# Self attention of a decoder layer: queries and keys projected in tiles of 128 tokens that run over batch borders

## What is computed

```python
# x: 8 batches x 224 tokens x 512; 16 heads of 64
x = rmsnorm(tokens) * norm_w
q, k, v = x @ Wq, x @ Wk, x @ Wv                 # heads split
q = q / max(norm(q), 1e-12) * (q_gamma + 1) * 8  # per token and head
k = k / max(norm(k), 1e-12) * (k_gamma + 1) * 8
sim = tanh(q @ k.T / 50) * 50 / 8
out = softmax(sim) @ v @ Wo                      # within a batch
x1 = layernorm(tokens + out)
```

## Time and profile before

| what | us |
|---|---|
| three executions | 1809.39, 1807.59, 1807.08 |
| their median | 1807.59 |
| the profiled execution | 1808.88 |
| its span, first to last instruction | 1806.4 |
| PE busy in the span | 1752.7 (97%) |
| DVE, ACT, POOL busy | 1412.5, 1172.5, 1113.4 |

### The profile page before, as it was taken

How to read it: one execution, slowest core, us unless ns; L and a number is a source line. 1 busy time by engine, 2 the same in 40 slices (tenths; PEclk the granted TensorE clock), 3 DMA queues, 4 the chain that set the end, 5 groups by cost and what they waited for, 6 DMA issues and landing times.

```text
span 1806.4 us, 37455 instructions
## 1 busy us (share of the span) xinstructions
PE 1752.7 (97%) x13942; PEld 1475.7 (82%) x13957; DVE 1412.5 (78%) x3240; ACT 1172.5 (65%) x2680; POOL 1113.4 (62%) x1250
## 2 busy tenths in 40 slices
PE   8999999999998899999999999999999999988997
PEld 7777777778877899999999999899899999974443
DVE  6777778787887677777777788777776777787888
ACT  6878887756755566666666667666666656654664
POOL 3434445664566586786686655677777788551554
PEclk9999999999998999999999999999999999999999
DMA  5223323111105423432432523314313341543553
GB/s 206 76 67 94 103 75 111 46 32 46 48 22 173 137 90 98 152 100 77 153 103 74 167 97 86 112 49 125 96 61 101 96 114 52 125 106 92 129 129 97
DMA packets 141106, 176.80 MB, mean 98 GB/s; under 512 B 63884, under 2 KB 99088, under 8 KB 140928
## 3 DMA queue, kind: packets, MB, share of 16 engines
q1 hardware_dynamic: 122392, 138.15, 25.3%
q0 software_dynamic: 14656, 28.92, 5.9%
q10 hardware_dynamic: 3880, 7.35, 1.3%
HBM read 109.25 MB, written 50.46 MB: 88 GB/s over the span
## 4 chain that ended last, share of the span: by engine, by line
PE 74%; DVE 10%; ACT 5%; POOL 5%; DMA 3%; issue 3%; ACTq 0%; POOLq 0%; DVEq 0%
PE att_ps_T L552 7%; PE att_ps_SA L1755 5%; PE att_ps_P L1731 5%; PE att_ps_SB L612 4%; PE att_ps_P L1719 4%; PE att_ps_P L552 4%; PE att_ps_P L1783 4%; PE att_ps_SB L600 3%; PE att_ps_O L1719 3%; PE att_ps_T L1719 3%; PE att_ps_P L1769 3%; PE att_ps_T L1731 3%; PE att_ps_O L1731 2%; PE att_ps_P L1794 2%; POOL sa_p_lo L423 2%
## 5 line engine op out<-in xcount | busy, mean ns | idle before, releaser
L1537 POOL TENSOR_TENSOR ca_pr<-ca_pr,ca_rec 112x750 f32<-112x750 f32 x256 | 366.6, 1453 | 187.2 <-DVE ca_rec L2017 184.3
L423 POOL TENSOR_TENSOR sa_p_lo<-sa_pr,sa_p_hi 112x448 fp32r<-112x448 f32 x128 | 146.8, 1162 | 210.5 <-ACT sa_p_hi L718 209.7
L1902 ACT ACTIVATE ca_big<-att_ps_P 126x384 fp32r<-126x384 f32 (+1 forms) x254 | 105.3, 449 | 66.1 <-PE att_ps_P L1769 64.9
L1896 ACT ACTIVATE ca_pr<-att_ps_SA,ca_nmax 112x750 f32<-112x750 f32 x128 | 113.7, 888 | 22.0 <-DVE ca_nmax L2013 11.2
L887 DVE RECIPROCAL sa_sums<-sa_sums 128x224 f32<-128x224 f32 x64 | 99.1, 1548 | 33.8 <-ACT sa_sums L727 33.6
L2022 DVE TENSOR_TENSOR ca_big<-att_ps_P,ca_big 126x384 fp32r<-126x384 f32 (+1 forms) x254 | 119.8, 498 | 6.2 <-ACT ca_big L1902 5.9
L2013 DVE TENSOR_REDUCE ca_nmax<-att_ps_SA 112x1 f32<-112x752 f32 x128 | 119.1, 931 | 1.3 <-PE att_ps_SA L1755 1.2
L2013 DVE TENSOR_REDUCE ca_nmax<-att_ps_SB 112x1 f32<-112x752 f32 x128 | 119.1, 930 | 0.0
L1731 PE MATMUL att_ps_P<-ca_w_hi,ca_ct 128*126 128x256 f32 x558 | 114.2, 284 | 1.4 <-DVE ca_q_lo L1996 1.4
L1896 ACT ACTIVATE ca_pr<-att_ps_SB,ca_nmax 112x750 f32<-112x750 f32 x128 | 113.3, 885 | 0.1
L1769 PEld LDWEIGHTS att_ps_P<-att_ident,ca_pr 64*126 64x126 f32 (+1 forms) x1524 | 85.5, 138 | 15.2 <-issue 10.8
(11 more groups left out here) (354 smaller groups left out, 6618.9 us busy)
## 6 DMA issues: line engine op xcount, KB each, us to landing
ct_kept<-ca_ct SPq DMA_DIRECT2D x8, 1134.0 KB, 9.3
ca_ct<-ct_kept POOLq DMA_DIRECT2D x8, 1134.0 KB, 7.7
ct_kept<-ca_ct SPq DMA_DIRECT2D x8, 1116.0 KB, 12.3
ca_ct<-ct_kept POOLq DMA_DIRECT2D x8, 1116.0 KB, 10.0
sa_xin<-in_x_dram SPq DMA_DIRECT2D x16, 448.0 KB, 3.7
xt_kept<-ca_xt SPq DMA_DIRECT2D x8, 896.0 KB, 5.2
ca_xt<-xt_kept POOLq DMA_DIRECT2D x8, 896.0 KB, 5.3
ternary<-ca_stage SPq DMA_DIRECT2D x36, 172.0 KB, 1.9
```

The costliest lines, as they stand in the source:

```text
L423: pool.tensor_tensor(p_lo[:, h % NB, :], pr[:, h % NB, :], f32(p_hi[:, h % NB, :]), ALU.subtract).then_inc(p_split, 1)
L1537: pool.tensor_tensor(w, w, rec[:, h % PB, c:c + 1].to_broadcast([R, S]), ALU.mult).then_inc(norm_done, 1)
L1896: act.activation(pr[:, h % PB, c, :].rearrange("r (a s) -> r a s", a=2), two_halves(psum[slot]), ACT.Exp, bias=nmax[:, h % PB, c:c + 1], a ...
```

## The change

Queries and keys are projected in tiles of P = 128 tokens counted over all 8 batches of a group, so four batches (896 tokens) are 7 tiles instead of 8. Within each four, the batches take up tiles [0, 1], [2, 3], [4, 5] and [6] (`TILES_OF`); for the fourth (batches 3, 7, 11, 15) the units Q1 and K1, their squares, sums, links of the norm and scalings are left out, and the engine only advances the semaphore. Values stay in tiles of 112 tokens of one batch.

- A tile can reach into the next batch. So x is transposed one batch earlier: AHEAD is 3, X and its splits are +++, and Q1 also waits for the next batch's XT0 and XT1. xt_hi and xt_lo become rings of two batches (448 columns and 64 more; the 64 are a second copy of the start of batches 2, 6, 10, 14, `wraps`).
- q_hi, q_lo, k_hi, k_lo become rings of two batches. T writes 128 columns per tile. For batches 1, 5, 9, 13 the two tiles run over the ring's end, and each copy is two pieces (`RING_PIECES`).
- guard is per tile, so the squares ss of the rows must come into the tiles' partitions: SP moves them with 3 or 4 small DMAs per batch in group 0 (`spread_squares`) ahead of the load of the next x, and DVE makes the guards from them in a new item U++ of its table (`guards`). guard is kept for group 1.
- sq has 2 places for 4, th 2 for 4, p_lo is written in the place of pr.
- The first two weight blocks' w_lo and gammas move on DVE from ahead of HQ0 of batch 0 to ahead of XT0 of batch 1; loads of group 1's first two weight blocks move on SP from behind x[1] to behind x[2].

```diff
-    AHEAD = 2
+    AHEAD = 3
+    PERIOD = 4
+    XW = 2 * N + HALF
+    TILES_IN = PERIOD * N // P
+    TILE_COLUMNS = [[0, P], [2 * P, 3 * P], [HALF, HALF + P], [2 * P + HALF]]
+    TILES_OF = [[0, 1], [2, 3], [4, 5], [6]]
+    TILES_READY = [[0], [1, 2], [3, 4], [5, 6]]
+    RING_PIECES = [[(0, 0, 2 * P)], [(0, 2 * P, P + HALF), (P + HALF, 0, HALF)], [(0, HALF, 2 * P)], [(0, 2 * P + HALF, P)]]
...
+        def spread_squares(m):
+            for c, r, n, t, row in pieces_of(m):
+                sp.dma_start(tile_ss[row:row + n, t:t + 1], ss[r:r + n, m % 2, c:c + 1]).then_inc(ss_spread, 16)
...
         def load_rows(src, before):
             if before:
+                sp.wait_ge(ss_done, before(2, 2))
+                if number(before) < B:
+                    spread_squares(number(before))
                 sp.wait_ge(filled[slot["XT1"]], filled_count("XT1", before))
-                sp.wait_ge(ss_done, before(2, 2))
...
             if b == 1:
                 load_weights(0, range(2, 4))
+            elif b == 2:
                 load_weights(1, range(2))
...
+            if u[0] != "V" and c >= len(tiles(at)):
+                pe.sem_inc(filled[slot[u]], 1)
+                return
...
+            if u == "Q1":
+                for t in range(2):
+                    pe.wait_ge(drained[slot[f"XT{t}"]], drained_count(f"XT{t}", lambda per, k: at(per, k) + per))
...
-                mm = pe.matmul(ps(u)[0:R, :], xs[:, k, c * R:c * R + R], ws[i][:, k, :],
+                mm = pe.matmul(ps(u)[0:rows, :], xs[:, k, col:col + rows], ws[i][:, k, :],
...
-                for c in range(2):
-                    mm = pe.transpose(ps(u)[:, i * N + c * R:i * N + c * R + R], t[:, c, p * P:p * P + P], ident[0:R, 0:R])
+                for c in range(len(tiles(at))):
+                    col = (2 * i + c) * P
+                    mm = pe.transpose(ps(u)[:, col:col + P], t[:, c, p * P:p * P + P], ident[:, :])
...
-            act.activation(q_hi[:, p, :], ps(u)[:, 0:N], ACT.Copy).then_inc(t_hi_done, 1)
+            for start, to, width in RING_PIECES[number(at) % PERIOD]:
+                q = act.activation(q_hi[:, p, to:to + width], ps(u)[:, start:start + width], ACT.Copy)
+            q.then_inc(t_hi_done, 1)
...
+            if wraps(u, at):
+                act.activation(xt_hi[:, :, 2 * N:XW], x_blocks(u)[:, :, 0, :], ACT.Copy)
...
+            dve.wait_ge(ss_spread, spread_count(m))
+            dve.tensor_scalar(guard[:, of], tile_ss[:, of], 1e-24 / DM, 1e-24 * RMS_EPS, ALU.mult, ALU.add).then_inc(guard_done, 1)
...
-                        if name == "HQ0":
-                            weights_lo(0)
-                            weights_lo(1)
-                            gammas()
-                        elif name == "G":
+                        if name == "G":
                             small_weights()
+                    if isinstance(b, int) and g * B + b + n == 1 and name == "XT0":
+                        weights_lo(0)
+                        weights_lo(1)
+                        gammas()
```

211 lines of the change are left out of this document (143 added, 68 removed).

## The result

The changed kernel takes 1830.11 us (median of four executions, 1824.19 to 1835.74), the kernel before beside it 1808.49. The ratio is 1.0115, 95% interval 1.0096 to 1.0135. The direction was forecast; 1816.5 was not the size, and the range ended at 1826. The profiled execution took 1830.53 us with a span of 1828.7, 22.3 more than before.

A forecast was written before the change was run, and what follows sets the result against it. In self attention the chain S3, ACT, POOL, O7 was taken to be as long as PE's stretch and to set it. Terms -9.9 + 3.1 + 8.8 + 2 + 5 = +9.0 us, forecast 1816.5 beside 1807.59, range 1803 to 1826.

The forecast's parts named there:

- The tiles, -9.9: Self attention's four steps without Q1 and K1: only K1's absence pays, 2.7 us each in group 0, 2.25 in group 1.
- V0 starts at 123.89 where K1 starts now: Step 2 of group 0: without K1, V0 takes its start time and Y0 has no stall, gain 2.7 us.
- The clock, +5: Four new PE gaps of some 2.2 to 2.7 us likely bring half clock: 5 us lost (0 to 12).
- Pieces and copies, +3.1: Copies of q and k split at the ring's end, 2.1 us, and extra x copies, 0.25 each: 3.1 lost (0 to 6).
- The start, +8.8 and +2: Kernel's start: waits on small DMAs, weights and x[2] delay K0's square, 8.8 us; K1 at half clock adds 2.
- (d): Start: ACT does x[2]'s squares ahead of Q0's and K0's, so K0's square ends at 26.5, not 17.74: 8.8 us.
- Term (a): Start: DVE waits for three small DMAs ahead of copying wnorm (at 10.7), holding ACT's first weight split, now at 7.22.
- term (e): Start: PE idles from about 22 to K1 at 30.8, so K1 runs at half clock: 2 us lost (0 to 2.8).
- The first: Rival: the clock holds in the short steps' gaps, +4.0 us, 1811.6; chance 0.15.
- The second: Rival: cheap start, small DMAs pass the weights, K1 stays fast, 6.5 us for 10.8, 1812.3; chance 0.12.
- The third: Rival: ACT or POOL serve heads 6 and 7 sooner, PE gains all 22.2 us, 1799.3; chance 0.08.
- The fourth: Rival: long clock falls behind the gaps, +12 us for +5, 1823.6; chance 0.10.

The follow-up runs named there:

- b4: Kernel before, Q1 and K1 of batches 3, 7, 11, 15 left out, ones in Q1's place, K0 scaled ahead of the third pair in group 1's short steps; 1809.32 us.
- b5: Same as b4, but the tiles left out are those of batches 2, 6, 10 and 14; 1802.11 us.
- e7: Changed kernel with ones in Q1's place and, in group 1's short steps, DVE scaling K0 right behind Q0; 1826.43 us.
- e1: Changed kernel plus ten matmuls of ones on PE wherever Q1 does not exist; 1829.39 us.
- b2: Kernel before, Q1 and K1 of batches 3, 7, 11, 15 left out, ten matmuls of ones in each missing Q1's place; 1809.99 us.
- b3: Kernel before, with ACT's and DVE's copies of q and k of batches 1, 5, 9, 13 each done in two pieces; 1810.97 us.
- e3: Changed kernel, with ACT taking the squares of x[2] behind batch 0's first V copy, not ahead of Q0's and K0's first squares; 1823.15 us.
- e5: e4 plus DVE scaling K0 right behind Q0 in group 1's short steps, and 20 more records of ones ahead of the first transposes of q; 1815.79 us.
- e6: e5 with POOL making the first two w_hi pieces for group 1's V weights behind the first head's p_lo in step 6; 1819.31 us.
- e4: Changed kernel with the edits of e1, e2 and e3 together, and the ones ahead of Q0 moved ahead of x[1]'s transposes; 1819.34 us.
- e2: Changed kernel, with DVE copying wnorm ahead of the guard of batch 0 instead of behind it; 1826.86 us.
- b1: Kernel before, Q1 and K1 of batches 3, 7, 11, 15 left out and nothing else; 1811.29 us.

## Why the prediction was right in direction and wrong in size

- *The tiles, -9.9.* Right in its mechanism for group 0, and Q1 is worth nothing: with the gap filled, O6 still waits for POOL and a short step gives 2.0 to 3.0 us (b4, b5; e7 2.3 to 3.0), never 5.5. In group 0 it holds, 2.7 forecast and 2.0 to 3.0 measured. In group 1 the step that failed is "V0 starts at 123.89 where K1 starts now", taken over with "stall 0.5, gain 2.25": I followed the data of V0 and Y0, and not the bank into which V0 writes. K0's scaling frees it, and with K1 gone nothing covers that. It cost 5.4 us for two steps, the fall of the clock behind the wait included (e1 to e7). That the wider matmuls cost nothing held: from 60 to 110 us those of 128 rows start every 0.235 us on average, as those of 112 do.
- *The clock, +5.* Filling the gaps is worth 5.0 us (e1), 4.2 in b2: the right term, and some luck in its size. All four gaps brought a fall where I had counted 3.2, they lasted 6.8 to 10.2 us and not 3.4, and a fall of 6.8 us cost 1.8 and 1.7 in group 0 where I had 3.1 for it. In group 1, where DVE's K0 was late anyway, a fall cost 1.1 and 0.4.
- *Pieces and copies, +3.1.* The ten full steps lost 4.6 without step 0's fall. The pieces are 1.3 of it (b3), less than the 2.1; the remaining 3.3 are in wider tiles and copies, for which I had 1.0. The prices of a split and of the wider copies were guesses for which the prediction gives no row, and this part was not taken apart.
- *The start, +8.8 and +2.* Measured 12.6, and 2.1 more for a fall in step 0. The chain was right up to K0's square (27.12 for 26.5) and its main link is (d) (e3: 5.4). Term (a) was right as an event and wrong as a cause: undoing it gives 0.9. Missing was the second guard on DVE, which takes 1.8 us on the way to the first transposes (42.67 for 41). Missing too was that Q0 now stands behind x[1] and the ones: it starts at 17.41 instead of 11.31, so PE idles 4.3 us ahead of K1 and not the 8.8 of term (e). Behind (d) this costs nothing; with (d) undone it is next (e3).
- *What was not in the sum.* The borders. Every step without a missing tile was taken to keep its length but for the copies. Step 7 took 1.6 us in the changed kernel, and mostly takes 3 to 5 when step 6 gives what it should (2.8 to 4.8 in b2, b4, e1, e5, e7; 2.6 in e6, 0.2 in e4); the landing of x, with the clock behind it, takes 3 to 5 where step 14 is shorter by 1 us or more (b4, e4 to e7). b5 shows that this is the place and not the work: 7.9 us faster with as many tiles missing, 9.2 from the four steps.
- *Rivals.* The first (the clock holds) is out, 30.7 us in the short steps ran at half clock. The second is out: wnorm came at 10.32 for 10.7, not at 9.3. The three small DMAs landed at 9.60, 9.79 and 10.23, the weight block, issued 4.3 us or more ahead of them, at 9.68. The prediction took the queue to be in order, which it is not: in e2 three small DMAs issued behind Wo landed at 20.81, 21.06 and 21.32, and Wo at 21.57. The Trainium skill's page "DMA: Bandwidth & Descriptors", section "Queues, rings and completion order", allows that, and these rows agree. So small DMAs do pass a block here, by 0.1 to 0.8 us, but at the start they took 2.9 to 3.6 us to land and not the 1.9 of that rival. (The prediction prices it at 1.4 us in one place and at 8.8 less 6.5, 2.3, in another, and does not say why.) The third is out: O6 waits 2.2 to 2.6 us for POOL's p_lo, and b1, which has neither start nor pieces, is not faster. The fourth, long falls, was the nearest in mechanism, but its 12 us were 5.

Of 22.3 us, the forecast has 9.0; of the missing 13.3 the short steps are 4.5, the start 1.8, full steps 3.6 with step 0's fall, step 7 1.6 and the end 1.9 (rounded).

One difference has nothing to do with the edits. S1 of batch 0 comes 2.1 to 2.3 us earlier in b2, b4 and b5 than in the kernel before, b1 and b3: the ones ahead of Q0 run at twice the pace there. Busy time from 6.8 to 9.0 us in the kernel before and in b4, PE first:

```profile
6.80:9.00 2.20, 2.20 (x11) 2.20 (x11) 2.10 (x7) 2.20 (x5) 0.00 (x0) 1.00 1.05 409
6.80:9.00 2.20, 2.20 (x20) 2.20 (x21) 2.15 (x7) 2.20 (x5) 0.00 (x0) 1.00 1.07 415
```

11 records in one and 20 in the other, one every 0.21 us and one every 0.11; where the granted clock is 1.00, as from 25.89 in the changed kernel, they start every 0.11. So PE runs at its slow clock in the first. (The granted clock of the first row is no help, its record begins at 11.1.) Step 0 takes 0.9 to 2.5 us of it back. Why the fast clock comes sooner in some executions stays open.

What stays open besides: whether the tiles can be laid out so that the short batch is not the one ahead of a border. With a tile of 128 tokens the sixth tile spans batches 2 and 3, so the layout fixes batch 3; that was not tried. No version that computes the reference beat the kernel before.

## What to carry over

Work taken off the busiest engine is worth what the chain beside it leaves, so follow three things past the cut: the data, the buffer that the next instruction writes, and the loads that were started before it. In this kernel a cut kept what it gained only where no load or engine with its own schedule met the work within a step behind it; ask where the next such meeting is, and cut ahead of an ordinary step. Where the cut leaves PE idle for 2 us, fill the gap, with real work if there is any: here the gap itself cost nothing, since another engine was awaited, and the slow clock behind it 0.4 to 1.8 us.

## What the runs showed of the hardware

- Idle gaps of PE of 2.2 to 2.7 us ahead of O6 in the short steps brought half clock every time, four each in the changed kernel, b1, e2 and e3, for 3.4 to 10.2 us; a gap of 1.6 us ahead of V0, which begins 2 us behind ten matmuls of ones, did in five of six (e1, b2, e4). It is no rule of the length alone: the gap of 2.25 us ahead of the first transposes (42.67 in the changed kernel) left the clock at 1.00 in the changed kernel, e1, e2, e3 and e7, and not in e4. With the gap ahead of O6 cut to 0.38 us by matmuls of ones, which move nobody's data, the clock held at 1.00.
- A stretch of 6.8 us at half clock cost 1.8 and 1.7 us in steps where PE had little else to wait for (steps 2 and 6, changed kernel against e1), one of 3.4 us 1.1 (step 2 of e2).
- The same two DVE instructions took 1.40 us where POOL was idle beside the first, and 2.9 to 4.9 beside a busy POOL (kernel before, e4, e5, b4, changed kernel), and POOL's two p_lo 2.24 to 3.17. e4 and e5, the same there but 1.1 us apart, took 2.90 and 4.03: the phase sets it, and a change far upstream sets the phase.
- A DMA of 4-byte elements that moves 0.1 to 0.4 KB costs SP's queue 0.6 us to issue, 28 of them in all; the x behind four of them went out 2.5 us later.
